# Transposes moved from TensorE to DMA, and routing moved into the next slot, in a decoder layer's second half

## The reference

```python
x = layernorm(x + self_attention(x))             # 16 heads of 32, causal
x = layernorm(x + cross_attention(x, ctx_1024))  # 16 heads, 77 context rows
x = layernorm(x + moe(x))

# moe: 8 experts, each 512 -> 256 -> 512, the best two of a row
logits = (x/|x|) @ (centroids/|centroids|).T + x @ w_route
gates  = softmax(where(logits >= second largest, logits, -inf))
out    = sum_e gates[e] * (gelu(x @ w1[e] + b1[e]) @ w2[e] + b2[e])
```

## Time and profile before

| what | value |
|---|---|
| time, median of 3 runs | 2477.39 us (2475.32 to 2479.24) |
| profiled execution, its own time | 2481.22 us |
| its span | 2479.3 us |
| mean granted clock of TensorE | 0.981 |
| PE busy | 2369.9 us (96%), 13612 instructions |
| PEld busy | 999.6 us (40%) |
| DVE busy | 1598.4 us (64%) |
| ACT busy | 1182.2 us (48%) |
| POOL busy | 1089.5 us (44%) |
| DMA | 155.05 MB in 130478 packets, mean 63 GB/s |

### The profile page before, as it was taken

How to read it: one execution, slowest core, us unless ns; L and a number is a source line. 1 busy time by engine, 2 the same in 40 slices (tenths; PEclk the granted TensorE clock), 3 DMA queues, 4 the chain that set the end, 5 groups by cost and what they waited for, 6 DMA issues and landing times. The chain is left out here.

```text
span 2479.3 us, 36649 instructions
## 1 busy us (share of the span) xinstructions
PE 2369.9 (96%) x13612; PEld 999.6 (40%) x13612; DVE 1598.4 (64%) x3854; ACT 1182.2 (48%) x2197; POOL 1089.5 (44%) x441
## 2 busy tenths in 40 slices
PE   7999799999999999999996899999999999999998
PEld 3444222323232323233333454554455454545443
DVE  4443487777777777777724476757566765757564
ACT  4232146666666666666654242443435343443431
POOL 0000259999999999999942112120212112021100
PEclk9999799999999999999998899999999999999999
DMA  7874502121312121322100501010100101010000
GB/s 246 282 253 161 132 6 74 32 74 32 74 32 74 32 74 31 74 70 69 32 19 13 184 1 65 1 48 18 34 32 1 65 1 50 16 48 18 1 18 17
DMA packets 130478, 155.05 MB, mean 63 GB/s; under 512 B 19854, under 2 KB 98190, under 8 KB 129277
## 3 DMA queue, kind: packets, MB, share of 16 engines
q1 hardware_dynamic: 130301, 152.72, 20.0%
HBM read 99.99 MB, written 52.17 MB: 61 GB/s over the span
## 5 line engine op out<-in xcount | busy, mean ns | idle before, releaser
L787 ACT ACTIVATE probs<-st_ps 128x512 f32<-128x512 f32 (+3 forms) x1280 | 611.8, 535 | 357.9 <-PE st_ps L901 199.7
L654 POOL TENSOR_TENSOR total<-total,probs 128x2048 f32<-128x2048 f32 (+3 forms) x190 | 667.6, 3514 | 47.3 <-ACT probs L787 27.9
L836 DVE TENSOR_REDUCE seg_max<-s_ps 128x1 f32<-128x512 f32 x768 | 506.2, 685 | 142.8 <-PE s_ps L887 140.6
L1558 PE MATMUL fps<-x2T,w_p_hi 128*128 128x512 f16 x1024 | 320.0, 381 | 0.0
L1558 PE MATMUL fps<-w_p_hi,hT 128*128 128x512 f16 x1024 | 306.1, 381 | 2.8 <-DVE x L1506 1.7
L840 DVE CUSTOM_DVE_ANT_0 s_ps<-s_ps,later 128x384 f32<-128x384 f32 (+3 forms) x512 | 249.0, 499 | 65.8 <-issue 65.7
L1305 ACT ACTIVATE hidden<-fps,keep_b_sb 128x512 f32<-128x512 f32 x128 | 87.7, 685 | 345.0 <-PE fps L1558 342.3
L1227 POOL TENSOR_TENSOR keep_soft<-keep_soft,ssum 128x1232 f32<-128x1232 f32 x32 | 71.6, 2248 | 400.1 <-DVE ssum L1397 400.1
L887 PE MATMUL s_ps<-keep_work,keep_soft 96*128 96x512 f16 (+3 forms) x640 | 221.4, 364 | 21.4 <-DMA keep_soft<-q_parts 11.3
L1510 DVE SCALAR_TENSOR_TENSOR x<-fps,gates_un,x 128x512 f32<-128x512 f32 x256 | 182.2, 743 | 89.0 <-PE fps L1558 86.9
L901 PE MATMUL st_ps<-keep_soft,keep_work 98*128 98x512 f16 (+3 forms) x640 | 221.4, 356 | 10.7 <-ACT probs L787 3.7
(11 more groups left out here) (200 smaller groups left out, 3611.7 us busy)
## 6 DMA issues: line engine op xcount, KB each, us to landing
keep_soft<-xT_in SPq DMA_DIRECT2D x8, 1024.0 KB, 6.1
q_parts<-qk_out SPq DMA_DIRECT2D x32, 256.0 KB, 3.6
k_parts<-qk_out SPq DMA_DIRECT2D x32, 256.0 KB, 4.2
keep_work<-w_in SPq DMA_DIRECT2D x8, 1024.0 KB, 8.6
v_rows<-v_out SPq DMA_DIRECT2D x32, 256.0 KB, 2.1
w_parts<-piece_cut SPq DMA_DIRECT2D x8, 1024.0 KB, 5.9
inv<-inv_rows SPq DMA_DIRECT2D x32, 256.0 KB
o_parts<-o_out SPq DMA_DIRECT2D x32, 256.0 KB, 2.6
```

The costliest lines, as they stand in the source:

```text
L654: last = nc.gpsimd.tensor_tensor(summed[:, :, off:], other[:, :, off:], probs[:, k % NP, :, off:], ALU.add)
L787: nc.scalar.activation(probs[:, k % NP, h, off:], st_ps[:, p % (2 * NVU) % RING, off:], ACT.Exp, scale=SCALE).then_inc(exp_done.sem, 1)
L836: nc.vector.reduce_max(highest, s_ps[:, slot], AX.X).then_inc(s_read.sem, 1)
L1558: last = nc.tensor.matmul(bank, lhs(a, t), rhs(b, t), start=(n == 0), stop=(n == len(steps) - 1))
```

## The change

It touches the second half in five places.

1. `turn1` and `turn2` leave TensorE. ScalarE and VectorE split the normed rows where they lie in SBUF, into `row_parts` (which lies in the upper part of `soft`); then SyncE issues four transposing DMA transfers a stage, one for each block of 128 rows (128 x 1024 fp16, 256 KB), straight into `x1T` or `x2T`. `query` and the routing products wait for `turn_done`.
2. The routing products become the first unit, `route`, of the next slot, where the chunk's experts run, in a bank of the experts. VectorE's choice stands at that unit; ScalarE's Exp stands behind hidden unit (0,1), VectorE's gates behind the lower half of hidden unit (1,0).
3. The units `gate` and `bias` move behind the first expert's four `expert` units, which now wait for the gates themselves.
4. `PLAN` puts 16 units ahead of `query` instead of 9, and 9 behind `out2` instead of 15. In the first slot three units (`UNITS_FIRST`) stand ahead of `out`.
5. The next rows are loaded from ScalarE's queue, in `norm2`. At the start SyncE issues the second chunk's rows behind the first `turn2` and all second-product weights behind the rows. In `first_chain` the stages from `query` on stand two positions later.

```diff
-    USES = (["dve"] * TT + ["dve"] * TT + ["act"] * KT + ["dve"] * (TT * NG)
-            + ["act"] * HG + (["act"] * HG + ["dve"]) * (NG - 1) + ["dve"] + ["dve"] * TT + ["dve"] * TT
-            + ["dve"])
-    AT_OUT, AT_T1, AT_Q = 0, TT, 2 * TT
+    USES = (["dve"] * TT + ["act"] * KT + ["dve"] * (TT * NG)
+            + ["act"] * HG + (["act"] * HG + ["dve"]) * (NG - 1) + ["dve"] + ["dve"] * TT)
+    AT_OUT, AT_Q = 0, TT
...
-    UNITS = []
+    UNITS = [("route", 0, 0)]
     for e in range(E + 1):
-        UNITS += [("hidden", e, n) for n in range(2) if e < E] + [("gate", 0, 0)] * (e == 0)
-        UNITS += [("bias", 0, j) for j in range(TT) if e == 1] + [("expert", e - 1, j) for j in range(TT) if e > 0]
+        UNITS += [("hidden", e, n) for n in range(2) if e < E] + [("expert", e - 1, j) for j in range(TT) if e > 0]
+        UNITS += [("gate", 0, 0)] * (e == 1) + [("bias", 0, j) for j in range(TT) if e == 1]
     NUNIT = len(UNITS)
...
+    UNITS_FIRST = 3
...
-    PLAN = [("out", 1), ("norm1", 3), ("turn1", 5), ("query", 1), ("scores0", 2), ("scores1", 7), ("scores2", 6),
...
+    PLAN = [("out", 2), ("norm1", 1), ("turn1", 13), ("query", 1), ("scores0", 2), ("scores1", 7), ("scores2", 6),
...
+            ("pv2", 3), ("pv3", 1), ("out2", 4), ("norm2", 1), ("turn2", 4), ("route", 0)]
...
+    row_parts = soft[:].rearrange("p j h s -> p (j h s)")[:, TT * D:2 * TT * D].bitcast(F16).rearrange(
+        "p (j s n) -> p j s n", j=TT, s=2)
...
+            def turn(i, u, which):
+                dst = x2T[parity(u)] if which else x1T
+                for j in range(TT):
+                    sp.wait_ge(lo_ready.sem, at(lo_ready, i, u, which * TT + j))
+                    sp.dma_start(dst[:, :, :, j * P:(j + 1) * P].rearrange("p s t n -> p (s t) n"),
+                                 row_parts[:, j].rearrange("p s n -> p (s n)"),
+                                 transpose=True).then_inc(turn_done, 16)
...
-                for dst, src in weights[1]:
-                    sp.dma_start(dst, src).then_inc(w2_loaded[0], 16)
-                load_next(-1, 1)
-                for dst, src in weights[2]:
-                    sp.dma_start(dst, src).then_inc(w2_loaded[1], 16)
+                turn(-1, 1, 1)
+                sp.wait_ge(turn_done, turned_at(0, 1))
+                load_rows(sp, S, x_rows, o_parts, 1)
+                load_context(1)
+                for part, loaded in zip(weights[1:], w2_loaded):
+                    for dst, src in part:
+                        sp.dma_start(dst, src).then_inc(loaded, 16)
                 for i in range(LOOPED):
                     for u in range(2):
-                        load_next(i, u)
+                        turn(i, u, 0)
+                        turn(i, u, 1)
...
                 if stage in ("turn1", "turn2"):
-                    k0, dst = (AT_T1, x1T) if stage == "turn1" else (AT_T2, x2T[p])
+                    src, done = (x1, 0) if stage == "turn1" else (x2[p], TT)
                     for j in parts:
-                        bank = wait_product(i, u, k0 + j)
-                        nc.scalar.activation(dst[:, 0, :, j * P:(j + 1) * P], bank.rearrange("p (t n) -> p t n", t=KT),
-                                             ACT.Copy, scale=XS).then_inc(hi_ready.sem, 1)
+                        act.wait_ge(normed.sem, at(normed, i, u, done + j))
+                        nc.scalar.activation(row_parts[:, j, 0], src[:, j], ACT.Copy,
+                                             scale=XS).then_inc(hi_ready.sem, 1)
+                elif stage == "norm2" and 0 < chunk(i, u) < NC - 1:
+                    act.wait_ge(dve_read.sem, at(dve_read, i, u, nth(USES, AT_O + TT - 1)))
+                    load_rows(act, S, x_rows, o_parts, chunk(i, u) + 1)
+                    load_context(chunk(i, u) + 1)
...
+                    if (e, j) == (0, 1):
+                        act.wait_ge(routed.sem, at(routed, i, u, 8))
+                        nc.scalar.activation(weight[:], logit[:], ACT.Exp).then_inc(gate_exped.sem, 1)
...
+            def rows_lo(i, u, src, which, hi_index):
+                for j in range(TT):
+                    dve.wait_ge(hi_ready.sem, at(hi_ready, i, u, hi_index + j))
+                    nc.vector.scalar_tensor_tensor(row_parts[:, j, 1], src[:, j], XS, row_parts[:, j, 0], ALU.mult,
+                                                   ALU.subtract).then_inc(lo_ready.sem, 1)
...
+            def route(i, u, f):
+                dve.wait_ge(norm_rooted.sem, at(norm_rooted, i, u, 0 - norm_rooted.per // 2))
+                dve.wait_ge(f_ready.sem, at(f_ready, i, u, f))
...
+            def gate(i, u):
+                dve.wait_ge(gate_exped.sem, at(gate_exped, i, u, 0))
+                nc.vector.tensor_tensor(weight[:], weight[:], chosen[:], ALU.mult).then_inc(routed.sem, 1)
...
+                    if (e, j) == (1, 0):
+                        gate(i, u)
...
-                elif stage in ("turn1", "turn2"):
-                    k0, src, done = (AT_T1, x1, 0) if stage == "turn1" else (AT_T2, x2[p], TT)
-                    for j in parts:
-                        pe.wait_ge(normed.sem, at(normed, i, u, done + j))
-                        bank = chain_bank(i, u, k0 + j)
-                        for t in range(KT):
-                            cols = slice(t * P, (t + 1) * P)
-                            last = nc.tensor.transpose(bank[:, cols], src[:, j, cols], ident[:])
-                        last.then_inc(c_ready.sem, 1)
                 elif stage == "query":
-                    pe.wait_ge(dve_read.sem, at(dve_read, i, u, nth(USES, AT_T1 + TT - 1)))
+                    pe.wait_ge(turn_done, turned_at(chunk(i, u), 0))
...
+                if kind == "route":
+                    pe.wait_ge(turn_done, turned_at(2 * i + u, 1))
+                    for r in range(TT):
+                        last = product(bank[:, r * 2 * E:(r + 1) * 2 * E],
+                                       lambda a, t: x2T[u][:, a, t, r * P:(r + 1) * P],
+                                       lambda b, t: W["route_p"][b][:, t], KT)
```

More of the change, by code:

```diff
@@ L1035, in chains @@
     VALUE = ("probs0", "probs1", "pv0", "probs2", "pv1", "probs3", "pv2", "pv3")
-    value_at = [(87 + n, stage) for n, stage in enumerate(VALUE)]
+    value_at = [(89 + n, stage) for n, stage in enumerate(VALUE)]
     first_chain = {
[L1038 to L1046, removed]
+        "sp": [(-40, "load"), (31, "turn")],
+        "pool": [(-100, "rows"), (12, "out"), (62, "scores1"), (68, "scores2"), (74, "scores3")] + value_at,
+        "act": [(24 + j, "turn1", j) for j in range(TT)] + [(39 + 3 * o, "query", o) for o in range(KT)]
+        + [(59, "scores0"), (65, "scores1"), (69, "scores2"), (73, "scores3")] + value_at,
+        "dve": [(-2, "out"), (14, "norm1"), (24, "turn1"), (52, "scores0"), (58, "scores1"), (64, "scores2"),
+                (68, "scores3")] + value_at,
+        "pe": [(4 * j - 2, "out", j) for j in range(TT)] + [(36 + 3 * o, "query", o) for o in range(KT)]
+        + [(52, "scores0"), (58, "scores1"), (64, "scores2"), (68, "scores3")] + value_at,
     }
@@ L1130, in slot @@
             def slot(i, u, with_chain=True, with_experts=True, start=0):
-                units_first = (i, u) == (0, 0)
+                ahead = UNITS_FIRST if (i, u) == (0, 0) else 0
+                if with_experts and experts:
+                    for f in range(ahead):
+                        experts(i, u, f, *UNITS[f])
                 for n, stage in enumerate(STAGES):
-                    if with_chain and n >= start and not (n == 0 and units_first):
+                    if with_chain and n >= start:
                         chain(i, u, stage)
                     if with_experts and experts:
-                        for f in range(FROM[n], FROM[n] + FILL[n]):
+                        for f in range(max(FROM[n], ahead), FROM[n] + FILL[n]):
                             experts(i, u, f, *UNITS[f])
-                    if with_chain and n == 0 and units_first:
-                        chain(i, u, stage)
                 if with_experts and finish:
@@ L1177, in store, with first @@
                              x2[u][:]).then_inc(stored[u], 16)
+            def first(what):
+                if what == "load":
+                    load_context(0)
+                else:
+                    turn(-1, 1, 0)
             def rest():
@@ L1615, in chain @@
                     last.then_inc(c_ready.sem, 1)
-                elif stage == "route":
-                    pe.wait_ge(dve_read.sem, at(dve_read, i, u, nth(USES, AT_T2 + TT - 1)))
-                    bank = chain_bank(i, u, AT_R)
-                    for j in range(TT):
-                        last = product(bank[:, j * 2 * E:(j + 1) * 2 * E],
-                                       lambda a, t: x2T[p][:, a, t, j * P:(j + 1) * P],
-                                       lambda b, t: W["route_p"][b][:, t], KT)
-                    last.then_inc(c_ready.sem, 1)
```

(5 more changed lines are left out.)

153 lines of the change are left out of this document (75 added, 78 removed).

## The result

| kernel | median of its runs, us | profiled execution, us (span) |
|---|---|---|
| before | 2478.15 (2475.28 to 2480.82, 9 runs) | 2481.22 (2479.3) |
| after | 2484.48 (2481.39 to 2486.72, 9 runs) | 2481.39 (2479.6) |

The ratio is 1.0026 (95% interval 1.0016 to 1.0037): +6.3 us, between +4.0 and +9.2. The two profiled executions do not show that difference, since that of before is 3 us above its median and that of after the fastest of nine. So the profile is read in pieces, each from one mark to the next inside one execution.

What follows compares the result with a forecast made beforehand. TensorE was taken to bound the slots. Start +7.8, six periods -3.9 and end +2.9 gave +6.8 us on 2477.4: 2484; range 2466 to 2520 overall, 2474 to 2495 for this case alone.

Steps and rivals of the forecast that it cites:

- Removed work: In each slot two turn stages of 16 transposes leave TensorE: 3.50 us less.
- The wait inside a slot: TensorE waits 0.8 us at gate and 0.8 at bias, third bias product late: 2.0 us a slot come back.
- The clock: Low clock behind each slot's new waits: between nothing and 1.69 us, half taken, 0.85 a slot.
- T: Time from a turn stage's last lower half to its last transfer's landing: 6 us, bounded by 2.1 and 15.9.
- C: Rival: slow transfers in series, T near 15.9, waits in middle slots; +61 us, 2539; chance 0.20.
- The slots hide the transfers: In middle slots query has 13 us of slack and routing 11, so T of 6 causes no wait.
- The start: Second half's start, where nothing hides T: query at 1435.3 against 1427.5, a loss of 7.8 us.
- The end: Last slot: routing waits 5.4 us, clock loss 1.69 behind it; 8.0 against 5.1 before, a loss of 2.9.
- A: Rival: short transfers, T = 2.1 at start and end; 2476, or 2471 if the clock holds; chance 0.20.
- B: Rival: no wait at the gate in the slots, chain shorter by 2 us; -11.2 us, 2466; chance 0.16.
- the sign named for A: At the start: the first routing product beginning before 1392 would show A instead of the forecast.

Runs made afterwards that it cites:

- e5: Changed kernel with the turn stages' transposes back on TensorE, the rest of the change kept; 2501.32 us, 1.0082 of the kernel before.
- e8: Changed kernel with VectorE's gates moved behind the lower half of hidden unit (0,1), bias units left in place; 2477.96 us in one run.
- e2: Changed kernel with gates behind hidden unit (0,1)'s lower half and bias units behind the next two hidden units; 2475.06 us, 0.9985 of before.
- e3: Changed kernel with out ahead of the first slot's units and the next rows loaded ahead of the transfers; 2469.84 us, 0.9962 of before.
- e4: Changed kernel with each transposing transfer cut in two of 128 KB, eight issues a stage; 2502.05 us, 1.0087 of before.
- e6: Changed kernel with the edits of e2 and e3, bias units two and two behind the two hidden units; 2454.95 us, 0.9903 of before.
- e9: The kernel before again, no edit, for a second profile; 2479.62 us in one run.
- e1: The changed kernel again, no edit, for a second profile; 2487.02 us, 1.0031 of before.
- e7: e6 with three units moved from in front of query to behind turn2; 2514.90 us, 1.0141 of before.

## Why the prediction was right

The forecast was 2484, with +6.8 us; measured were 2484.48 and +6.3.

**Removed work: right.** 3.5 us a slot leave TensorE, and e5, which has them back, is 142.94 where the changed kernel is 139.38: 3.56. TensorE's busy time there is 3.7 us higher (141.01 against 137.30) and its idle time nearly the same (1.9 against 2.1), though the waits are not the same ones.

**The wait inside a slot: right in place and size.** Two waits of 0.8 us and a late third bias product, 2.0 in all: the profile has 0.83 released by the first expert sum and 0.78 by the gate copy, the four bias products take 1.16 instead of 0.86, 1.91 in all; and a period is 139.38, which is 140.90 - 3.50 + 1.98. The first sum stood at 17.55 in the forecast; it ends 17.7 us after `out` (1562.00 + 0.76 against 1545.07). The chain too: Exp behind hidden (0,1), upper halves, table load, gelu, gates, first sum. e8 took the first wait away, e2 both, and the time went with them.

**The clock: mechanism right, size off.** The term was half of 1.69, 5.1 us over six slots. The loss came in 2 of 6 periods in each of the four profiles that have both waits (the changed kernel twice, e3, e4), 1.5 each: 3.0. The slots gained 6.1 instead of 3.9. That is the mis-sized term. It came in no period of e2, e5, e6 and e8, which don't have both waits together.

**T: right in size, wrong in its reason.** From the last lower half (1382.99) to the last landing (1388.67) 5.7 us, against 6. But I built it from a landing of 4.2 and queueing; it is 1.34 us of SyncE for each issue, in series, and 3.4 behind the last. That the packets are of 256 bytes fits (in the page of after 87438 packets are under 512 B, in that of before 19854: 1056 more for each of the 64 transfers, where 1024 were reckoned), but not that they would go one transfer after the other at 3.9 us (C). The Trainium skill, "VectorE: DVE Perf Modes", section "The three transpose paths", has 1309 ns for one 128x128 block by DMA; by an estimate from it a stage of 32 blocks in series would take 42 us. The trace disagrees with that estimate: 32 blocks landed within 7.5 us of the first issue (1381.21 to 1388.67). What one block alone takes, no run here shows.

**The slots hide the transfers: right.** No query and no route of a middle slot waits, and with eight issues (e4) the periods stay.

**The start: +7.8 forecast, +8.1 measured, with two errors that nearly cancel.** The two positions in the attention's tail were put at 1.5, and what the first chunk's transposes give back by leaving it was put at nothing, without a reason. On the whole tail nothing shows (from SyncE's issue at 1096.80 to out2 267.5 us before, from 1092.57 267.4 after). In its pieces both do: from the stored piece issued at 1263.88 to that at 1311.51 are 47.6 us before, 46.4 and 46.8 in the two profiles of after, and 48.2 in e5, which has the transposes back; from there to the second half's first issue 52.8 before and 53.1 in e9, 54.1 and 53.6 after, 53.7 in e5. Inside the start, the norm's rows and the landing came within 0.3 us of the forecast, but VectorE could not add out's results at once: it stood behind the routing, which needs the norms' root, which POOL made only after its bias (1403.31 + 1.02). The norm began 54.3 us after out2's first matmul instead of 53.2.

**The end: +2.9 forecast, +2.4 and +4.5 in the pairs of profiles.** The wait of 5.4 was 4.74, the clock loss behind it about 1.5 (granted 0.85 from 2380 to 2390 us). On the side of before the sum took 1.69 for the clock from a single profile; e9 has the same wait and no loss, and that is most of what parts the two pairs.

**The rivals.** A fell on the landing at 5.7 instead of 2.1; B on the waits, which are there; C on the middle slots. Read by the time alone, the sign named for A did come: the first routing product begins at 1388.81, before 1392. But that execution reaches the second half 4.4 us early; e1, which reaches it at 1364.32 as before did, has 1392.67, and its transfers too land 5.5 us behind the last lower half. That the transfers are the culprit fell with e5, that the difference lies ahead of the second half with e1 and e9.

**The total is closer than its terms.** The pieces add up to +5.5; the slots are 2.2 us better than forecast, the start and the end together 0.9 worse, and the errors inside the start nearly cancel. That +6.8 came within half a microsecond of the median is in part luck: the interval alone is 5 us wide.

Open is why the clock is lost in two of six slots, which all have the same two waits.

## What to carry to other kernels

Work taken off a full engine is worth only what the waits put in its place leave: here 3.5 us a slot left and 2.0 came back, because VectorE made the gates behind a lower half whose gelu stood behind the Exp, `turn1`'s upper halves and two table loads on ScalarE, both engines with time to spare. So follow the moved step through every queue that it joins. Look at both ends of a pipeline by themselves: a latency that every middle slot hides showed in the first and the last one, and moving independent work (`out`, with its loads) into it gave 15 to 17 us, over twice what the whole change had cost. In a plan where several engines run one written order, moving units for one engine's sake changes what meets what on the others (e7).

## What had not been expected of the hardware

A transposing transfer keeps the issuing queue for 1.3 us, whether it moves 256 or 128 KB (1.34 and 1.30), where the plain ones issued behind it at the start mostly took 0.4 to 0.6. And the granted clock fell behind two waits of 0.8 us that lie 0.6 us apart in 8 of 24 such periods (the changed kernel twice, e3, e4), but in none of 12 where the first of the two was missing (e5, e8); a single wait of 1.67 us was followed by the low clock in one profile of before and by the full one in the other.
